# A graph attention kernel in which SP brings one tile of source rows in every fourth node block, a row a transfer, in place of a gather on GpSimd

## What is computed

```python
h = layernorm(x)                                   # 12500 x 256
xp = (h @ W).reshape(n, 4, 64)
a_src, a_dst = (xp * att_src).sum(-1), (xp * att_dst).sum(-1)
alpha = leaky_relu(a_src[src] + a_dst[dst], 0.2)
ex = exp(alpha - segment_max(alpha, dst)[dst])
w = ex / segment_sum(ex, dst)[dst]
agg = segment_sum(xp[src] * w[..., None], dst)     # the row of each edge's source
x1 = x + elu(agg.reshape(n, 256) + bias)
# then: LN, weights = x1n @ wr + br, the top half by weight gets
# (gelu(x1n @ w1 + b1) @ w2 + b2) * weight, added to x1n + x1
```

## Time and profile before

| | us |
|---|---|
| runs | 2191.46, 2186.37, 2186.64 |
| median | 2186.64 |
| profiled execution, its time | 2193.97 |
| profiled execution, its span | 2192.2 |
| POOL's gathers, first to last start | 129.5 to 2095.6 |

### The profile page before, as it was taken

How to read it: one execution, slowest core, us unless ns; L and a number is a source line. 1 busy time by engine, 2 the same in 40 slices (tenths; PEclk the granted TensorE clock), 3 DMA queues, 4 the chain that set the end, 5 groups by cost and what they waited for, 6 DMA issues and landing times.

```text
span 2192.2 us, 29093 instructions
## 1 busy us (share of the span) xinstructions
PE 1883.2 (86%) x9507; PEld 1547.8 (71%) x9508; DVE 1533.1 (70%) x3416; ACT 1154.9 (53%) x1672; POOL 1525.6 (70%) x1626
## 2 busy tenths in 40 slices
PE   8945888898899889888888888889889889888887
PEld 6734777777677777777777776767677777777775
DVE  5556776677677667767767777777667667777776
ACT  4543555555555555555555555555555555555533
POOL 2367777777777777777777777777777777777710
PEclk9977999999999999999999999999999999999988
DMA  8854455455455555554555555455545545555457
GB/s 281 296 167 136 134 145 146 133 146 146 136 142 146 146 137 142 146 141 133 146 146 137 142 146 146 138 140 147 146 132 145 146 135 142 144 147 138 135 226 284
DMA packets 157136, 340.11 MB, mean 155 GB/s; under 512 B 46645, under 2 KB 73937, under 8 KB 155698
## 3 DMA queue, kind: packets, MB, share of 16 engines
q0 software_dynamic: 75088, 208.19, 35.0%
q1 hardware_dynamic: 74706, 116.59, 16.7%
q10 hardware_dynamic: 7184, 13.41, 1.6%
HBM read 299.38 MB, written 38.68 MB: 154 GB/s over the span
## 4 chain that ended last, share of the span: by engine, by line
POOL 49%; issue 22%; PE 12%; DMA 11%; ACT 3%; DVE 1%; POOLq 1%; DVEq 0%; SPq 0%; ACTq 0%
POOL rows L710 49%; DMA rows<-node_rows,ends 10%; PE ag_ps L972 4%; ACT rows L854 3%; PE ag_ps L1097 2%; PE y_ps L1080 2%; PE h_ps L1061 2%; POOLq L410 1%; PE ag_ps L1168 1%; PE ag_ps L1169 0%; DVE rows L1443 0%; DMA steps_of_rows<-in_L_gnn_att_dst 0%; DMA selfr<-in_dst,edge_block 0%; PE xl_ps L1001 0%; PE tr_ps L1001 0%
## 5 line engine op out<-in xcount | busy, mean ns | idle before, releaser
L710 POOL DMA_INDIRECT rows<-node_rows,ends x1563 | 1484.1, 950 | 493.2 <-issue 449.9
L1097 PE MATMUL ag_ps<-rows,oh 128*128 128x260 f32 x3518 | 835.4, 398 | 26.1 <-DVE rows L1443 25.6
L1097 PEld LDWEIGHTS ag_ps<-rows,oh 128*128 128x128 f32 x3518 | 690.3, 200 | 172.6 <-DVE rows L1443 51.8
L1061 PE MATMUL h_ps<-xnT,w1s 128*128 128x256 f32 x1568 | 457.1, 443 | 215.9 <-DVE zz L1424 201.1
L1443 DVE TENSOR_TENSOR rows<-rows,xl_ps 128x512 f32<-128x512 f32 (+3 forms) x392 | 503.1, 1346 | 47.2 <-ACT rows L874 47.2
L1061 PEld LDWEIGHTS h_ps<-xnT,w1s 128*128 128x128 f32 x1568 | 327.7, 217 | 291.6 <-DVE zz L1424 209.8
L1080 PE MATMUL y_ps<-w2s,hT 128*128 128x256 f32 x1568 | 368.8, 384 | 11.5 <-DVE oh L1405 7.6
L1080 PEld LDWEIGHTS y_ps<-w2s,hT 128*128 128x128 f32 x1568 | 296.2, 191 | 71.6 <-DVE oh L1405 25.9
L1424 DVE TENSOR_TENSOR zz<-rows,edge_dm 128x72 f32<-128x72 f32 x98 | 22.8, 233 | 447.8 <-DMA rows<-node_rows,ends 432.7
L854 ACT COPY rows<-rows 128x780 f32<-128x780 f32 x97 | 81.6, 842 | 403.5 <-DMA rows<-node_rows,ends 403.5
L1405 DVE TENSOR_TENSOR oh<-xl_ps,dloc 128x2304 f32<-128x2304 f32 x98 | 249.0, 2541 | 0.0
(11 more groups left out here) (245 smaller groups left out, 1528.9 us busy)
## 6 DMA issues: line engine op xcount, KB each, us to landing
spare<-dst SPq DMA_DIRECT2D x97, 288.0 KB, 4.7
rows<-node_rows,ends POOLq DMA_INDIRECT x1563, 2.9
selfr<-node_rows SPq DMA_DIRECT2D x98, 130.0 KB, 3.0
base<-in_x SPq DMA_DIRECT2D x14, 896.0 KB, 7.0
base<-in_x SPq DMA_DIRECT2D x49, 256.0 KB, 3.3
ffn_rows<-yb ACTq DMA_DIRECT2D x48, 256.0 KB, 4.8
node_rows<-base SPq DMA_DIRECT2D x13, 910.0 KB, 5.5
base<-in_x_turned SPq DMA_DIRECT2D x14, 384.0 KB, 7.5
```

The costliest lines, as they stand in the source:

```text
L710: pool.indirect_dma_start(out=rows[:, b, t, :], out_offset=None, in_=table, in_offset=bass.IndirectOffsetOnAxis(ap=ends[:, b, t, 0:1], axi ...
L1061: last = nc.tensor.matmul(h_ps[:, m * PAIR:(m + 1) * PAIR], w1s[:, c, n * P:(n + 1) * P], xnT[:, c, :], start=(c == 0), stop=(c == DC - 1))
L1097: product = nc.tensor.matmul(ag_ps[b][:, 0:ROW], oh[:, b, t, :], rows[:, b, t, :], start=(t == 0), stop=False)
```

## The change

In 23 blocks (6, 10, 14, ... 94: `staged_blocks`) POOL skips the gather of tile 9 (`STAGED`). SP brings these 128 rows, in the four blocks before: one transfer of the tile's 128 sources to one partition of SBUF, then in each of four turns four loads of eight registers and 32 transfers of one row, whose address comes from a register, to a staging place of 128x260. There are two such places, in the unused `xrow` and in a free part of `spare`, used in turn. In the staged block ACT copies the place into tile 9 of `rows`, ahead of its copy of the last tile. The waits for the number of gathers are counted anew (`given`, `given_up_to`), and some semaphores that nobody or few waited for are left out or merged (`ex_ok`, `selfx_ok`, `minus_ok`, `d16_st`, `win_st`) to make room for the new ones.

```diff
+    STAGED, EVERY, FIRST_STAGED = 9, 4, 6
+    staged_blocks = [w for w in range(FIRST_STAGED, NW - 1) if (w - FIRST_STAGED) % EVERY == 0]
+    ROWS_A_TURN = P // EVERY
+    AT_ONCE = 8
+
+    def given(w):
+
+        return TILES - 3 - (w in staged_blocks) if w < NW - 1 else LAST - 3
...
+        stage = [xrow[:, :], spare[:, 5 * D:5 * D + ROW]]
+        sources = [xoh[0:1, :].bitcast(I32), spare[0:1, 5 * D + ROW:5 * D + ROW + P].bitcast(I32)]
...
                 sp.dma_start(selfr[:, b, :], table[bass.ds(w * P, P), :]).then_inc(ld_self[b], 16)
+                if sp_extras is None:
+                    stage_rows(w)
...
+            def stage_rows(w):
+
+                n, turn = divmod(w + EVERY - FIRST_STAGED, EVERY)
+                if n >= len(staged_blocks) or w + EVERY < FIRST_STAGED:
+                    return
+                k = n % 2
+                if turn == 0:
+                    if n == 0:
+                        sp.wait_ge(parts_ok, 1)
+                    tile = in_edges(entry(sp, staged_blocks[n], 0, NCH - TILES) + STAGED)
+                    with nc.allow_non_contiguous_dma("the sources of a tile's edges to one partition"):
+                        sp.dma_start(sources[k], edges[:, bass.ds(tile, 1), 0].rearrange("p t -> t p")).then_inc(src_ld, 16)
+                    if n >= 2:
+                        sp.wait_ge(moved, n - 1)
+                    sp.wait_ge(src_ld, 16 * (n + 1))
+                for at in range(turn * ROWS_A_TURN, (turn + 1) * ROWS_A_TURN, AT_ONCE):
+                    _, nodes_of = nc.values_load_multi_w_load_instructions(
+                        sources[k][:, at:at + AT_ONCE], engines=[mybir.EngineType.SP], min_val=0, max_val=NW * P - 1,
+                        skip_runtime_bounds_check_because="an edge's source is one of the nodes")
+                    for j, node in enumerate(nodes_of):
+                        sp.dma_start(stage[k][at + j:at + j + 1, :], table[bass.ds(node, 1), :]).then_inc(row_ld[k], 16)
...
-                    gather(t, gath[b])
+                    if not (pool_extras is None and w in staged_blocks and t == STAGED):
+                        gather(t, gath[b])
...
+            def move_staged(w, b):
+
+                n = staged_blocks.index(w)
+                act.wait_ge(row_ld[n % 2], 16 * P * (n // 2 + 1))
+                act.wait_ge(freed[GROUPS - 1], w - 1)
+                nc.scalar.copy(rows[:, b, STAGED, :], stage[n % 2]).then_inc(moved, 1)
...
+                if act_extras is None and w in staged_blocks:
+                    move_staged(w, b)
...
+                    dve.wait_ge(gath[b], 16 * given_up_to(w))
+                    if w in staged_blocks:
+                        dve.wait_ge(moved, staged_blocks.index(w) + 1)
```

More of the change, by code:

```diff
@@ L91, in build, with given_up_to @@
     last_in_group = {min((g + 1) * FREED, TILES) - 1 if g < GROUPS - 1 else TILES - 1: g for g in range(GROUPS)}
+    STAGED, EVERY, FIRST_STAGED = 9, 4, 6
[4 more added lines that the diff above has]
+        return TILES - 3 - (w in staged_blocks) if w < NW - 1 else LAST - 3
+    def given_up_to(w):
+        return sum(given(v) for v in range(w % 2, w + 1, 2))
     with ExitStack() as ctx:
@@ L239, in build @@
         ROOMS = len(yin)
+        stage = [xrow[:, :], spare[:, 5 * D:5 * D + ROW]]
+        sources = [xoh[0:1, :].bitcast(I32), spare[0:1, 5 * D + ROW:5 * D + ROW + P].bitcast(I32)]
+        assert FLAT // 2 + 4 <= 5 * D and 5 * D + ROW + P <= 7 * D
         chunks = []
@@ L349, in build @@
         y_ld = [sem(f"y_ld{k}") for k in range(ROOMS)]
+        src_ld, row_ld, moved = sem("src_ld"), sem2("row_ld"), sem("moved")
         def bc(v, n):
@@ L847, in store @@
                 act.dma_start(by_partition(y_dram, 2 * p, 2), yb[:, :, :]).then_inc(y_st, 16)
+            def move_staged(w, b):
[3 more added lines that the diff above has]
+                nc.scalar.copy(rows[:, b, STAGED, :], stage[n % 2]).then_inc(moved, 1)
             def carry(w, i, b):
-                act.wait_ge(gath[b], 16 * (TILES - 3) * (i + 1))
+                if act_extras is None:
+                    act.wait_ge(gath[b], 16 * given_up_to(w))
+                else:
+                    act.wait_ge(gath[b], 16 * (TILES - 3) * (i + 1))
                 if known(w, 1):
@@ L870, in exponentials @@
                 act.wait_ge(diff_ok, w + 1)
-                nc.scalar.activation(ex_ps[:, 0:tiles_of(w), :], diff[:, 0:tiles_of(w), :], ACT.Exp).then_inc(ex_ok, 1)
+                nc.scalar.activation(ex_ps[:, 0:tiles_of(w), :], diff[:, 0:tiles_of(w), :], ACT.Exp)
                 if not isinstance(w, int) or w < NW - 1:
@@ L923, in _ @@
             nc.scalar.preload_act_table_set(EXP_AND_LN)
-            act.wait_ge(minus_ok, 1)
+            act.wait_ge(loc_ok, 1)
             for w in range(2):
@@ L1421, in exponents @@
                 dve.wait_ge(dm_ok, w + 1)
-                dve.wait_ge(gath[b], 16 * ((TILES - 3) * i + n - 3))
+                if dve_extras is None:
+                    dve.wait_ge(gath[b], 16 * given_up_to(w))
+                    if w in staged_blocks:
+                        dve.wait_ge(moved, staged_blocks.index(w) + 1)
+                else:
+                    dve.wait_ge(gath[b], 16 * ((TILES - 3) * i + n - 3))
                 dve.wait_ge(gath_last[b], dve.to_reg(optional_landed(dve, w)))
```

23 lines of the change are left out of this document (11 added, 12 removed).

## The result

| | before | after |
|---|---|---|
| median, us | 2186.02 | 2206.63 |
| lowest to highest, us (10 runs each) | 2181.40 to 2191.46 | 2190.48 to 2210.32 |
| profiled execution, its time (its span) | 2193.97 (2192.2) | 2195.16 (2193.1) |

What follows compares the result with a forecast made beforehand. POOL's serial gathers were taken as the pace: 23 x 1.25 = 28.7 us saved, less 3 us of waits for TensorE, new SP and ACT work free, so 2186.6 - 25.7 = 2160.9 us; 8-in-10 range 2153 to 2310 us.

Steps and rivals of the forecast that it cites:

- What bounds the kernel before, and the gain: POOL's queue of gathers, 1.25 us each, sets the pace; 23 fewer save 28.7 us, 25.7 after waits for TensorE.
- the loss of 3: POOL in staged blocks: where TensorE is late, the saved gather is only waited away, 3 of 23 times, 3 us.
- ACT and DVE: ACT's added copy, 0.3 us, and DVE's wait for it cost 0, lying within more than 4 us of slack.
- A row: One-row transfer on SP: 0.42 us start to start, 0.23 of it the transfer; 32 rows take 13.5 us a turn.
- the rival of dear rows: On SP a row costs 0.53 us, the turn is 21.1 us and the time 2279 us; chance 0.06.
- The load of eight registers: On SP, eight registers come with one access at 0.35 us; four loads take 1.4 us a turn, 8.9 at the high end.
- The fetch of the sources: On SP each fourth turn: load, steps and a 2.0 us landing, 2.6 us together, 0.65 a turn.
- SP's old work: What SP already did each block outside its 17.9 us wait: 2.09 us, the mean of 1.85 and 2.33.
- The sum: SP's turn 2.09 + 0.65 + 13.5 + 1.4 = 17.6 us against a block of 19.7, leaving 2.1 to spare.
- registers one after the other: Rival on SP: each further register adds r, SP setting the pace beyond 0.075 us; slower by 7 to 460 us; chance 0.26.
- The lag: SP may fall 10 us behind before ACT, which reads the targets at 1032.17, has to wait for them.
- Traffic: One-row transfers load one DMA engine by at most 2.3 us in 19.7, to 0.60 busy; cost taken as 0.

Runs made afterwards that it cites:

- lower group: The faster of two groups of executions of the unedited changed kernel: three of its first ten, 2190.5 to 2195.2 us, the profiled one among them.
- upper group: The slower group of executions of the unedited changed kernel: seven of its first ten, 2204.6 to 2210.3 us, eleven of twenty in all; none was profiled.
- kernels with a shorter SP turn: Five variants of the changed kernel: sources fetched a turn early, sixteen registers a load, loads ahead of rows, early fetch with either; 21 to 26 us faster than before.
- early fetch: Changed kernel with the 128 sources fetched at the end of the turn before the one that uses them: 2166.47 us, ratio to before 0.9891.
- loads ahead: Changed kernel with a turn's four loads of eight registers moved ahead of its 32 one-row transfers: 2160.10 us, ratio to before 0.9890.

## Why the prediction was wrong

It forecast 2160.9 us and the kernel took 2206.6. The traces account for the way to 2195, the lower group; the last 11 us are the upper group's and open. The signs that the text set down for being wrong came: no wait of SP in front of the ends, POOL waiting for the ends and ACT for the targets. Its own steps, one by one:

- **What bounds the kernel before, and the gain.** Right. POOL's gathers were the pace; leaving 23 out gives 29.0 us (24 to 33), where 28.7 stood, and 25.7 with the loss of 3, which the runs neither show nor exclude. The kernels with a shorter SP turn come to 2160.1 to 2166.5, a gain of 21 to 26.
- **ACT and DVE.** Right that it costs nothing: the copy takes 0.39 us (0.3 predicted), and leaving it out moves nothing (2195.49 against 2195.17). That DVE would stand 34 us for it, with ACT held by late targets, the text had only as an if.
- **A row.** Right: 223 ns at SP, 0.40 us from start to start (0.23 and 0.42 predicted), 13.39 us a turn against 13.5. The transfer of win, one partition in the earlier trace rows, was the right row to take, and the rival of dear rows (0.53) falls.
- **The load of eight registers. This is the step that failed first**: 0.78 us against 0.35, which I had put at its low end "with less trust than the rest". Four of them take 3.19 us a turn in place of 1.4, and 1.8 of the 2.6 us are here. Half of it is the seven further registers (0.27 us for one, 0.53 for eight), half is that a load stands behind a one-row transfer (another 0.26).
- **The fetch of the sources**: 1.16 us a turn against 0.65. I took the median landing of the ends, 2.0 us, for a transfer that writes 128 words to one partition; it landed after 4.3 us, of which its issue took 0.576. 0.5 us of the 2.6. (The terms of this part add up to 2.5 and not 2.6; that is 0.03 a turn.)
- **SP's old work**: 2.51 us against 2.09. In the same 92 turns before it was 2.2, so 0.1 was in my reading of two turns for the mean. Nothing was added to it; but its one-register load now stands behind a row and takes 0.54 us (median 541 ns behind a row, 286 behind selfr). I had carried it over at the duration it had in another neighbourhood.
- **The sum.** 17.6 became 20.26, and 2.1 us of slack became a lack of 0.5. The threshold itself, POOL's turn of 19.7, was right (19.76 with the gather left out). The rival "registers one after the other" would have it decide at r = 0.075 us; measured between one and eight it is 0.037, and 28 x 0.037 = 1.0 us is too little by itself. The kernel went to the slow side because terms came together: with the error of the loads alone the turn is 19.4 and SP would still have fitted, and so with that of the fetch or of the old work alone; the loads with either of the others are past 19.7.
- **The lag.** I gave SP 10 us by which it may fall behind before anyone waits; the trace of the changed kernel shows 10.1 from the first to the last of the 92 turns. That the two agree so closely is in part luck: in the second half of the kernel the lag swings between about 8 and 15 us within groups of four turns, and with four registers at a load it grew by 14.4.
- **Traffic.** Right: gathers at 948 ns, and 2944 one-row transfers beside the gathers in the kernels at 2160.
- **The chances.** 0.56 for faster rested on a fit with 2.1 us to spare, in which every unknown had been taken at or near its low end. Errors of the unknown terms all point one way then. 2206.6 lies inside the wide range up to 2310, which took in two rivals at their prices; neither of them is what happened, registers at 0.037 us being half of their threshold, so that the range holds the time by its width.

The text weighed the Trainium skill, Runtime: NRT & Kernel Launch, Instruction fetch mechanics, with some 200 ns for each register in bulk. The runs show 0.037 us for a further register from one to eight and 0.056 from eight to sixteen, from SBUF: the direction in which that page spoke against the change was right, and its size, which it gives for loads from HBM, doesn't hold for these.

## What to carry to other kernels

Work given to an idle queue is free only up to that queue's turn, so add the turn up with each unknown at its middle: a sum that fits with 2 us of 20 to spare fits by nothing when four of its terms are at their low end. Where a queue waits for a small transfer whose content it needs, issue it a turn earlier, and load registers in one group ahead of the transfers that use them; each of these alone made 0.4 to 0.9% slower into 1.1% faster here. When a queue that nobody watched gets into the chain of waits, look first for who waits for its old duties (here the targets, 301 us, and the ends), then for its new ones. And take several runs beside the profile: here one profile was slower than all runs of its kernel, and the others came from the faster of two groups.

## What the runs showed of the hardware

- A register load on SP right behind a one-row transfer takes about 0.26 us longer than behind a load, a wait or a transfer over 128 partitions: one register 0.54 against 0.29, four 0.56 against 0.30, eight 0.79 against 0.53, sixteen 1.24 against 0.98. Right behind the fetch of the sources, also a transfer to one partition, eight took 0.54 (early fetch) and sixteen 1.26 in the median, so the one partition alone doesn't explain it. What the load waits for there the traces don't say.
- Of the registers themselves, four cost next to nothing over one (0.30 against 0.29), and from there on each costs some 0.056 us: 0.53 for eight, 0.98 for sixteen.
- A transfer of 1040 bytes from one row to one partition takes 223 ns of SP's queue, over 128 partitions 330 to 430 ns, and one of 128 single words from DRAM to one partition 576 ns with 4.3 us to landing (3.9 in the kernel with the loads ahead, 3.4 with sixteen registers a load).
